# A graph attention stage, from steps of two tiles to steps of four

## What is computed

```python
Q = _ln(h @ Wq[i], gq[i], bq[i]);  K = _ln(h @ Wk[i], gk[i], bk[i])
score = (Q[src] * K[dst]).sum(-1) + 0.1 * (edge_attr * Q[src][:, :40]).sum(-1) + logm[dst]
smax = segment_max(score, src);  es = exp(minimum(score - smax[src], 20.0))
denom = segment_sum(es, src);  alpha = es / (denom[src] + 1e-10)
aggi = segment_sum(alpha[:, None] * (h[dst] @ Wm[i]), src)
```

## Time and profile before

| | |
|---|---|
| median of 3 runs | 19432.3 us (19406.12 to 19461.73) |
| the profiled execution | 19381.23 us |
| its span | 19379.5 us |
| granted TensorE clock, mean over the span | 0.687 |
| the four attention stretches | 7545 to 8640, 9222 to 10312, 10870 to 11956, 12513 to 13616 us |

### The profile page before, as it was taken

How to read it: one execution, slowest core, us unless ns; L and a number is a source line. 1 busy time by engine, 2 the same in 40 slices (tenths; PEclk the granted TensorE clock), 3 DMA queues, 4 the chain that set the end, 5 groups by cost and what they waited for, 6 DMA issues and landing times. The chain is left out here.

```text
span 19379.5 us, 403631 instructions
## 1 busy us (share of the span) xinstructions
PE 10513.3 (54%) x119643; PEld 7960.3 (41%) x119643; DVE 11231.2 (58%) x26717; ACT 5238.7 (27%) x15775; POOL 9046.0 (47%) x10645
## 2 busy tenths in 40 slices
PE   1001046666666327875894796588255555534334
PEld 1001024444444116864784786578233333333213
DVE  6557034454444456885887788588433333366647
ACT  0000012222222004652562464266122222211110
POOL 7778654444444533431441343244355545465251
PEclk9855555555555559997997998899566666655556
DMA  4552334443445217544552754555111111134434
GB/s 131 175 179 75 97 75 73 73 73 73 73 73 73 48 29 236 162 131 158 163 164 76 225 164 108 193 160 163 38 45 41 44 42 43 39 107 140 132 119 153
DMA packets 1580320, 2116.07 MB, mean 109 GB/s; under 512 B 418326, under 2 KB 1234222, under 8 KB 1573225
## 3 DMA queue, kind: packets, MB, share of 16 engines
q1 hardware_dynamic: 1196382, 1438.64, 24.0%
q0 software_dynamic: 309216, 539.49, 14.7%
q10 hardware_dynamic: 74552, 135.95, 2.1%
HBM read 1290.57 MB, written 726.03 MB: 104 GB/s over the span
## 5 line engine op out<-in xcount | busy, mean ns | idle before, releaser
L686 POOL DMA_INDIRECT attend_rows<-key_rows,attend_fetch_now x1824 | 1752.9, 961 | 2331.7 <-PE attend_seg L1722 2003.6
L686 POOL DMA_INDIRECT edges_rows<-raw,edges_perm_now x1824 | 1764.8, 968 | 2008.2 <-issue 1635.7
L1766 ACT ACTIVATE attend_hot<-attend_lane_hot,attend_share 128x128 f32<-128x128 fp8e4 x7296 | 2227.2, 387 | 114.0 <-DVE attend_share L1789 74.0
L686 POOL DMA_INDIRECT mlp_xin<-table,mlp_staged x1564 | 1492.3, 954 | 1441.4 <-PEq L2313 981.0
L686 POOL DMA_INDIRECT keys_rows<-table,keys_staged x1564 | 1867.9, 1194 | 539.4 <-issue 539.4
L1722 PE MATMUL attend_seg<-attend_rows,attend_hot 128*128 128x49 f32 x14592 | 1839.7, 280 | 81.4 <-issue 43.5
L1722 PEld LDWEIGHTS attend_seg<-attend_rows,attend_hot 128*128 128x128 f32 x14592 | 1763.7, 197 | 126.8 <-issue 119.9
L1709 PE MATMUL attend_qx<-attend_table,attend_oht 128*128 128x90 bf16 x21888 | 1106.4, 208 | 412.9 <-DMA attend_oht<-src_hots 361.6
L692 POOL DMA_INDIRECT messages<-spread_out,spread_place_now x912 | 1013.0, 1111 | 606.4 <-issue 470.3
L1709 PEld LDWEIGHTS attend_qx<-attend_table,attend_oht 128*128 128x128 fp8e4 x21888 | 1010.4, 101 | 479.8 <-issue 477.9
L1806 DVE TENSOR_REDUCE attend_mraw<-attend_top 128x2 f32<-128x1024 f32 x912 | 1110.3, 1217 | 52.2 <-issue 28.7
(11 more groups left out here) (546 smaller groups left out, 23345.9 us busy)
## 6 DMA issues: line engine op xcount, KB each, us to landing
key_rows<-expand_out SPq DMA_DIRECT2D x304, 624.0 KB
attend_ea<-edge_attrs SPq DMA_DIRECT2D x912, 160.0 KB
tally_rows<-messages SPq DMA_DIRECT2D x152, 864.0 KB, 4.8
attend_table<-q SPq DMA_DIRECT2D x1832, 67.5 KB
expand_oht<-dst_hots SPq DMA_DIRECT2D x304, 384.0 KB
attend_oht<-src_hots SPq DMA_DIRECT2D x912, 128.0 KB
attend_lane_hot<-src_hots_by_edge SPq DMA_DIRECT2D x912, 128.0 KB
raw<-keys_rows ACTq DMA_DIRECT2D x46, 2176.0 KB
```

The costliest lines, as they stand in the source:

```text
L686: return nc.gpsimd.indirect_dma_start(out=out, out_offset=None, in_=table, in_offset=bass.IndirectOffsetOnAxis(ap=index, axis=0))
L1766: ins = nc.scalar.activation(hot[p][:, u, c, :], lane_hot8[r][:, u, c, :], ACT.Copy, scale=share[p][:, u, c:c + 1])
```

## The change

`attend` goes from pairs to steps of four tiles, 114 per layer, 456 in all. SP issues one `oht`, one `ea` and one `lane_hot` DMA per four tiles, each twice as large, and still four table DMAs. The turn, `parted`, `mb`, back, `arg`, the exponential and `share` are done once per four tiles; products, maxima and sums stay pieces of two tiles (half h = 0 or 1), with `prod`, `top` and `seg` as before. `across` moves from the spare end of `qx` into the bank of `back`. The slots are: `rows` six steps, `oht` three, `ea`, `lane_hot`, `table` and `turned` two. In `edge_pass` the copy into `k.sloc` goes, and so does its buffer.

The core of the diff:

```diff
-    LOOPS = PAIRN // RING
+    FOUR, TURN = 4, 6
+    SUPER = NS // FOUR
+    LOOPS = SUPER // TURN
...
             def _(sp):
-                def step(n, b, t):
+                def step(n, s, t):
                     if live(n, 0):
-                        at = bass.ds(n * 2, 2)
-                        sp.wait_ge(s_back, n + 1)
-                        sp.dma_start(ea[b][:], ...).then_inc(s_load[b], 16)
-                        sp.dma_start(oht[b][:], ...).then_inc(s_load[b], 16)
-                        sp.wait_ge(s_seg, n + 1)
-                        sp.dma_start(lane_hot[b][:], ...).then_inc(s_lane[b], 16)
-                        after(sp, s_q, n - 1)
-                        tables(n + 1, (b + 1) % 3)
+                        at = bass.ds(n * FOUR, FOUR)
+                        after(sp, s_back, n - 2)
+                        sp.dma_start(oht[s % 3][:], ...).then_inc(s_oht[s % 3], 16)
+                        after(sp, s_q, n * 2 - 2)
+                        for u in range(FOUR):
+                            block_i = sp.value_load(k.irow[0:1, bass.ds(n * FOUR + u, 1)], min_val=0, max_val=NT - 1)
+                            sp.dma_start(table[s % 2][:, u], ...).then_inc(s_tab[s % 2], 16)
+                        after(sp, s_score, n - 1)
+                        sp.dma_start(ea[s % 2][:], ...).then_inc(s_ea[s % 2], 16)
+                    if live(n, 2):
+                        after(sp, s_hota, n * 2 - 6)
+                        sp.dma_start(lane_hot[s % 2][:], ...).then_inc(s_lane[s % 2], 16)
...
             def _(pe):
+                    if live(n, 2):
+                        maxima(0)
+                    if live(n, 4):
+                        sums(n - 4, 4, 1)
+                    if live(n, 0):
+                        pe.wait_ge(s_oht[s % 3], nth(s, t, 0, 3) * 16)
+                        pe.wait_ge(s_tab[s % 2], nth(s, t, 0, 2) * (16 * FOUR))
+                        products(0)
+                    if live(n, 2):
+                        maxima(1)
+                    if live(n, 3):
+                        sums(n - 3, 3, 0)
+                    if live(n, 0):
+                        products(1)
+                    if live(n, 2):
+                        pe.wait_ge(s_most, n - 1)
+                        after(pe, s_arg, n - 2)
+                        ... 16 back matmuls of n - 2 ...
+                        ins.then_inc(s_back, 1)
+                    if live(n, 1):
+                        pe.wait_ge(s_score, n)
+                        after(pe, s_arg, n - 1)
+                        mm(across, spread_[(s - 1) % 2][:], k.identb[:], start=True, stop=True).then_inc(s_turned, 1)
...
             def _(act):
+                def step(n, s, t):
+                    scaled(n, s, t, 0)
+                    evict(n - 3, 1)
+                    scaled(n, s, t, 1)
+                    evict(n - 2, 0)
+                    ... turned of n, waits s_turned n + 1 ...
+                    ... exponential of n - 1, waits s_arg n ...
...
             def _(dve):
+                def step(n, s, t):
+                    products(0)
+                    ... share of n - 2 ...
+                    summed(0); highest(0)
+                    products(1)
+                    summed(1); highest(1)
+                    ... mb of n - 1; parted of n ...
+                    dve.wait_ge(s_back, n)
+                    ... arg of n - 1 ...
...
 edge_pass, vector:
-                    ch.step(v.tensor_copy(k.sloc[:, bass.ds(n * COL, COL)], r[:, :, SL]))
```

More of the change, by code:

```diff
@@ L1237, in _ @@
                 step(s, s, 0)
-            n0, per = ch.n, 20 * TURN
+            n0, per = ch.n, 19 * TURN
             with dve.Fori(1, LOOPS) as t:
@@ L1600, in attend @@
 def attend(nc, k):
-    LOOPS = PAIRN // RING
+    FOUR, TURN = 4, 6
+    SUPER = NS // FOUR
+    LOOPS = SUPER // TURN
+    WIDE = FOUR * GR
     with ExitStack() as ctx:
         ph = Phase(nc, ctx, "attend")
[L1605 to L1613, removed]
-        prod = ph.sb("prod", [P, 2, GR, QROW])
[L1615 to L1625, removed]
@@ new lines, in attend @@
+        two, three, ring = range(2), range(3), range(TURN)
+        oht = [ph.sb(f"oht{b}", [P, FOUR, W // 2], BF16) for b in three]
+        oht8 = [oht[b][:].bitcast(F8) for b in three]
+        ea = [ph.sb(f"ea{b}", [P, FOUR, GR * RBF]) for b in two]
+        rows = [ph.sb(f"rows{b}", [P, FOUR, GR * KROW]) for b in ring]
+        fetch_now = ph.sb("fetch_now", [P, TURN, FOUR], I32)
+        lane_hot = [ph.sb(f"lane_hot{b}", [P, FOUR, GR * P // 2], BF16) for b in two]
+        lane_hot8 = [lane_hot[b][:].bitcast(F8).rearrange("p u (c l) -> p u c l", c=GR) for b in two]
@@ new lines, in attend @@
+        table = [ph.sb(f"table{b}", [P, FOUR, 3, QROW], BF16) for b in two]
+        prod = ph.sb("prod", [P, 2, GR, QROW])
+        score = [ph.sb(f"score{b}", [P, FOUR, GR]) for b in three]
+        spread_ = [ph.sb(f"parted{b}", [P, P], BF16) for b in two]
+        parted = [a[:, 0:2 * WIDE].rearrange("p (h u c) -> p h u c", h=2, u=FOUR) for a in spread_]
+        turned, sel = [ph.sb(f"turned{b}", [P, P], BF16) for b in two], ph.sb("sel", [P, WIDE, P], BF16)
+        mraw = ph.sb("mraw", [P, FOUR])
@@ L1634, in attend @@
         ea4, rows4 = [by4(a[:]) for a in ea], [by4(a[:]) for a in rows]
[L1635 to L1639, removed]
+        back4 = back[:, 0:2 * WIDE].rearrange("p (u c m) -> p u c m", u=FOUR, m=2)
+        seg4 = seg[:, 0:4 * 64].rearrange("p (h u w) -> p h u w", h=2, u=2)
+        across = back[:, P:2 * P]
@@ L1640, in steps @@
+        def steps(eng, step, tail):
             for s in ring:
@@ L1643, in steps @@
                 for s in ring:
[L1644 to L1648, removed]
+                    step(t * TURN + s, s, t)
+            for s in range(tail):
+                step(SUPER + s, s, LOOPS)
+        live = lambda n, lag: not isinstance(n, int) or lag <= n < SUPER + lag
+        nth = lambda s, t, lag, slots: t * (TURN // slots) + (s - lag) // slots + 1
+        half = lambda h: slice(2 * h, 2 * h + 2)
         with nc.Block() as block:
@@ L1663, in step @@
                     if live(n, 4):
-                        p = (b - 4) % 3
                         pool.wait_ge(s_most, n - 3)
-                        nc.gpsimd.tensor_tensor(k.most[:, bass.ds((n - 4) * 2, 2)], mb[p][:, :, 0], mb[p][:, :, 1], ALU.add).then_inc(s_kept, 1)
-                steps(pool, step)
-                pool.wait_ge(s_kept, PAIRN)
+                        nc.gpsimd.tensor_tensor(k.most[:, bass.ds((n - 4) * FOUR, FOUR)], mb[(s - 4) % 3][:, :, 0], mb[(s - 4) % 3][:, :, 1], ALU.add).then_inc(s_kept, 1)
@@ L1671, in _ @@
+                steps(pool, step, 4)
+                pool.wait_ge(s_kept, SUPER)
             @block.sync
             def _(sp):
[L1673 to L1678, removed]
-                    if live(n, 0):
-                        at = bass.ds(n * 2, 2)
-                        sp.wait_ge(s_back, n + 1)
-                        sp.dma_start(ea[b][:], k.ea.rearrange("(p u) w -> p u w", p=P)[:, at, :]).then_inc(s_load[b], 16)
-                        sp.dma_start(oht[b][:], k.oht_s.rearrange("(p u) w -> p u w", p=P)[:, at, :]).then_inc(s_load[b], 16)
-                        sp.wait_ge(s_seg, n + 1)
-                        sp.dma_start(lane_hot[b][:], k.hot_s.rearrange("(p u) w -> p u w", p=P)[:, at, :]).then_inc(s_lane[b], 16)
-                        after(sp, s_q, n - 1)
-                        tables(n + 1, (b + 1) % 3)
@@ L1693, in _ @@
+                steps(sp, step, 2)
             @block.tensor
@@ L1695, in _, with products @@
                 mm = nc.tensor.matmul
-                pe.sem_inc(s_seg, RING)
-                pe.sem_inc(s_back, RING)
                 pe.wait_ge(s_sel, 1)
[L1700 to L1704, removed]
+                def step(n, s, t):
+                    def products(h):
+                        after(pe, s_prod, n * 4 - 2 + 2 * h)
                         pe.sem_inc(s_pe_turn, 1)
@@ L1812, in _ @@
+                    if live(n, 1):
+                        dve.wait_ge(s_back, n)
+                        ch.done(v.tensor_tensor(arg[1 - two_][:], score[one][:], back4[:, :, :, 0], ALU.subtract))
+                        v.tensor_tensor(arg[1 - two_][:], arg[1 - two_][:], back4[:, :, :, 1], ALU.subtract).then_inc(s_arg, 1)
                 for s in ring:
                     step(s, s, 0)
-                n0, per = ch.n, 6 * RING
+                n0, per = ch.n, 5 * TURN
                 with dve.Fori(1, LOOPS) as t:
@@ L2698, in program @@
             k.keep_u = bl("keep_u", [P, NS])
-            k.sloc = bl("sloc", [P, NS * GR])
             with ExitStack() as own:
```

194 lines of the change are left out of this document (110 added, 84 removed).

## The result

| | before | after |
|---|---|---|
| median of 3 runs | 19432.3 us | 22578.9 us (22555.0 to 22630.6) |
| ratio | | 1.1625, 95% interval 1.1598 to 1.1653 |
| span of the profiled execution | 19379.5 us | 22553.3 us |
| the four attention stretches | 4374 us | 7578 us |
| per four tiles (/ 456) | 9.59 us | 16.6 us |

What follows compares the result with a forecast made beforehand. SP's issue time bounds the kernel before; the change closes a loop of 7.9 + 5.4 us plus 1.3 for the clock, 14.6 against 9.59 us, x 456 = +2285, less 30, on 19432: 21690 us, range 20850 to 22700.

Steps and rivals of the forecast that it cites:

- named case: Attention: loop through SP with the clock falling briefly, 14.6 us per four tiles, 21690 us in all; chance 0.64.
- rival 3: Attention: clock low through every burst, 17.3 us per step, 22910 us in all; chance 0.1.
- What bounds the kernel before: Attention: SP's issue time is the bound, 4.80 us per pair; VectorE and TensorE stand some 10% behind.
- The loop: Attention, once per step: back, SP's issues, landing, TensorE's burst, back; 13.3 us before any clock term.
- SP's leg: Attention, from the end of back through SP's issues to the products' start: 7.9 us, between 7.1 and 9.6.
- TensorE's leg at the full clock: Attention: products, maxima, sums, products and back twice on TensorE, 5.4 us per step.
- rival 2: Attention: the clock stays up, 13.3 us per step, 21090 us in all; chance 0.2.
- The burst at the low clock: Attention: TensorE's products to back at the low level take 9.4 us, 4.0 more than at the full one.
- The clock term: Attention: a third of the low-clock burst's extra 4.0 us, 1.3 us per step; softest term, 0 to 4.0.
- The delay of `mb`: Attention: `mb` on VectorE could make back later, by at most 0.3 us.
- Rival 4: Attention: SP's issues cheap or loop hidden, TensorE needs 9.1 us per step, 19210 us in all; chance 0.05.
- The copy: First pass: removing the copy into `sloc` is hidden and gains 0, with 40 us as its bound.

Runs made afterwards that it cites:

- Experiment 5: Kernel before, with the lane_hot transfer issued by ACT in place of SP, along with its wait for the sums: 19227 us, ratio 0.9897.
- experiment 1: Also called e_order: changed kernel, with SP issuing the four table DMAs ahead of its wait for back and `oht`: 20347 us, ratio 1.0486.
- experiment 2: Changed kernel, with only two of the four tables loaded per step and all products using these two: 20870 us.
- experiment 4: Kernel before, in pairs, with SP waiting for back of three pairs before, not six, ahead of `ea` and `oht`: 22914 us.
- experiment 3: Changed kernel, with 28 idle matmuls per step on TensorE while it waits for the tables: 21714 us.

## Why the prediction was right, and which term was off

The direction, the mechanism and the range held: 22579 us lies in 20850 to 22700, but only 121 us below its upper end, 889 us above the 21690 that was named. That it fell inside owes something to luck: the four stretches are 1882 to 1901 us, where the prediction had 1600 to 1700 for its named case and 1950 for rival 3, most of which its range left out. By its steps:

- **What bounds the kernel before** was read rightly: SP's issue time. Experiment 5 shows it by taking one issue away, and the wait that belongs to it.
- **The loop** back, `oht` and tables, landing, burst, back is shown by SP's wait of 9.1 us at that line, by the 1486 us that the products waited for the tables, and by experiments 1, 2 and 4.
- **SP's leg**, 7.9 us: the turn above has 7.95, by terms 1.8 us from back to the first table (1.4 was taken), 3.8 to the fourth (4.2), and 2.3 from its start to the products (2.3), with 0.5 us for one issue. The mean over 444 steps is 8.65, 0.75 more than taken. It comes in ahead of `oht`: SP issues it 1.0 us after the end of back on average, where 0.2 was taken.
- **TensorE's leg at the full clock**, 5.4 us: 5.2 in experiment 3. So **rival 2's step of 13.3 us** is what experiment 3 ran at, 13.2.
- **The burst at the low clock**, 9.4 us: 9.3 in 184 of 444 steps.
- **The clock term** failed, the one called the softest. "The low stretch begins in the idle time and the dense burst ends it, so I take a third of that, 1.3 us": the bursts took 8.0 us on average, 2.6 of the 4.0 more than the leg at the full clock. Two steps in five had the low clock from products to back, and the others had part of it. That is 1.25 us of the miss of 2.0 us per step, and SP's leg the other 0.75. This part goes with the clock too: `oht` was issued 1.6 us after the end of back where the burst before was wholly low, 0.6 where it was partly low, and 0.27 in experiment 3 after bursts at the full clock (ends of matmuls are modelled; why the hand-over is later was not looked into). Together 2.0 us x 456 = 910 us, the whole miss. Rival 3 (every burst cold, 22910 us) was nearer than the named case.
- **The delay of `mb`**, "at most 0.3 us", is hidden in the changed kernel (back at 8327.80 follows the products without a gap), but it is 0.96 us in the round of e_order above (0.55 on average at the full clock): with SP's leg out of the way it becomes part of the bound. Rival 4's step of 9.1 us was thus a little short: 9.4 us is the average at the full clock. What rival 4 lacked was the clock, which in e_order was low in some or all of 255 rounds of 452.
- **The copy**, taken as 0, is 20 to 28 us: the first pass's steps, which were to keep their length, became 0.09 us shorter. Its cover on TensorE hides what comes after it in the same step, not the one-hots' way over SP and back for the next. That this is the path was only argued.

The Trainium skill, TensorE: Matmul & The Clock Gate (HAM oscillation), has each burst after a wait for DMAs start cold. Here this holds in part (the burst at 8321.80 started cold and was warm by the sums at 8325.04), and wholly in experiment 4. Its advice is to restructure the loop so that more work lies between two waits; experiment 3 shows that filling the wait also pays.

## What to carry to other kernels

When loads get larger slots, count how far back the oldest wait of the loading queue reaches, and what is queued behind it: here a wait on the newest work but three, with five transfers behind it (two of the pair's own in experiment 4), closed a loop in which no engine was full. Put first in the queue what is free first. And where such a loop leaves TensorE idle in every step, price the burst at the low clock as a likely case, not as the bad end: here it ran wholly low in experiment 4 (1.3 us idle per step), cost two thirds of the full penalty in the changed kernel (3.3 us idle), and struck more than half of the rounds even in experiment 1 (1.15 us idle).

## What the runs showed that was not expected

- TensorE can stay at the low level with 84% of the time busy: in experiment 4 it was busy 1661 of 1966 us at a clock of 0.50, with an idle time of 1.3 us in every 8.7. The kernel before, 89% busy, ran at 0.96. The slow clock makes the burst longer and TensorE busier, and yet the clock does not come back.
- Work that is thrown away made a kernel faster: 28 matmuls per step gave 865 us.
- With 28 more matmuls in the loop, TensorE stopped once in six steps for up to 5.2 us with no release shown. What it waited for stays open.
